# Attention operands stacked straight from the projection's SBUF tile, and the row of maxima put by ScalarE's queue

## The reference

```python
def proj(x, W, b):
    y = jnp.einsum('bsd,de->bse', x, W) + b
    return y.reshape(B, S, N_HEADS, D_K).transpose(0, 2, 1, 3)
q = proj(Q, W_Q, b_Q); k = proj(K, W_K, b_K); v = proj(V, W_V, b_V)
scores = jnp.einsum('bhqd,bhkd->bhqk', q, k) / jnp.sqrt(jnp.float32(D_K))
attn = jax.nn.softmax(scores, axis=-1)
out = jnp.einsum('bhqk,bhkd->bhqd', attn, v)
...
x = x + jnp.tanh(g_xattn[0]) * _L0_xattn_ref(_layernorm(x), ctx_1024, ctx_1024, W_Q, b_Q, ...)
x = x + jnp.tanh(g_ffn[0]) * _L0_ffn_ref(_layernorm(x), w_gate, w_up, w_down)
x = x + jnp.tanh(g_xattn[1]) * _L1_xattn_ref(_layernorm(x), ctx_1024)
x = x + jnp.tanh(g_ffn[1]) * _L1_ffn_ref(_layernorm(x), weight, bias, delta_w, delta_act)
```

## Time and profile before

| | |
|---|---|
| median of three runs | 1622.26 us |
| the profiled execution | 1623.71 us, with a span of 1621.9 us |
| TensorE busy (matmul) | 1477.0 us, 91% |
| VectorE busy | 1226.8 us, 76% |
| ScalarE busy | 875.9 us, 54% |
| GpSimd busy | 890.9 us, 55% |
| mean granted TensorE clock | 0.958 |
| bytes moved by DMA | 265.32 MB |

### The profile page before, as it was taken

How to read it: one execution, slowest core, us unless ns; L and a number is a source line. 1 busy time by engine, 2 the same in 40 slices (tenths; PEclk the granted TensorE clock), 3 DMA queues, 4 the chain that set the end, 5 groups by cost and what they waited for, 6 DMA issues and landing times. The chain is left out here.

```text
span 1621.9 us, 24716 instructions
## 1 busy us (share of the span) xinstructions
PE 1477.0 (91%) x6993; PEld 937.9 (58%) x6993; DVE 1226.8 (76%) x2135; ACT 875.9 (54%) x1433; POOL 890.9 (55%) x1148
## 2 busy tenths in 40 slices
PE   5699999999999889899784999999999968999997
PEld 3466666556565566655532455555555447887885
DVE  4867677777868677677662788888888848999986
ACT  4156666666565556555453555555555535555552
POOL 3166676585675757656462343343333316777775
PEclk9899999999999989999878999999999989999998
DMA  6757849485694865937941344444444653556522
GB/s 201 227 163 211 258 150 273 143 249 161 185 277 128 229 190 176 289 108 226 251 115 55 95 114 109 109 116 107 107 107 109 190 146 120 167 165 203 166 86 62
DMA packets 252172, 265.32 MB, mean 164 GB/s; under 512 B 139932, under 2 KB 162984, under 8 KB 247720
## 3 DMA queue, kind: packets, MB, share of 16 engines
q1 hardware_dynamic: 252072, 264.14, 57.4%
HBM read 149.50 MB, written 82.87 MB: 143 GB/s over the span
## 5 line engine op out<-in xcount | busy, mean ns | idle before, releaser
L724 ACT ACTIVATE a_probs<-a_sc 128x512 f32<-128x512 f32 x512 | 300.5, 595 | 288.5 <-PE a_sc L608 284.7
L843 DVE TENSOR_REDUCE a_negmax<-a_mx 128x1 f32<-128x512 f32 x512 | 339.0, 675 | 108.1 <-PE a_mx L591 107.3
L938 POOL TENSOR_TENSOR a_acc<-a_acc,a_probs 128x512 f32<-128x512 f32 x248 | 311.6, 1285 | 11.1 <-ACT a_probs L724 9.7
L938 POOL TENSOR_TENSOR a_acc<-a_probs 128x512 f32<-128x512 f32 x124 | 156.9, 1285 | 247.9 <-ACT a_probs L724 247.0
L591 PE MATMUL a_mx<-a_stack 96*128 96x512 f32 x512 | 231.0, 451 | 40.3 <-DVE a_negmax L843 22.3
L1089 PE MATMUL bank<-wcode,b_xq 128*128 128x512 bf16 x1024 | 229.3, 383 | 11.1 <-DMA b_xq<-b_xcode 11.1
L608 PE MATMUL a_sc<-a_stack 97*128 97x512 f32 x512 | 217.7, 427 | 21.0 <-DMA a_stack<-a_mrow 19.5
L1089 PEld LDWEIGHTS bank<-wcode,b_xq 128*128 128x128 bf16 x1024 | 100.5, 98 | 135.0 <-DMA b_xq<-b_xcode 12.5
L854 DVE RECIPROCAL a_attn<-a_den 128x128 f32<-128x128 f32 x128 | 120.8, 947 | 71.1 <-PE a_den L646 58.6
L591 PEld LDWEIGHTS a_mx<-a_stack 96*128 96x128 f32 x512 | 103.1, 201 | 114.4 <-DVE a_negmax L843 55.0
L1127 ACT ACTIVATE b_sig<-bank,b_tok 128x512 f32<-128x512 f32 x128 | 87.4, 683 | 94.0 <-PE bank L1089 91.9
(11 more groups left out here) (165 smaller groups left out, 2637.0 us busy)
## 6 DMA issues: line engine op xcount, KB each, us to landing
a_stack<-spill SPq DMA_DIRECT2D x192, 256.0 KB, 6.8
spill<-k_part SPq DMA_DIRECT2D x64, 512.0 KB, 3.5
ctx_t<-k_wo SPq DMA_DIRECT2D x16, 1024.0 KB, 9.8
c_ct<-ctx_t SPq DMA_DIRECT2D x8, 2048.0 KB, 7.9
a_stage<-in_x_dram SPq DMA_DIRECT2D x32, 256.0 KB, 5.1
a_stage<-in_ctx_dram SPq DMA_DIRECT2D x32, 256.0 KB, 3.1
a_wsum<-in_L_ffn_w_gate_dram SPq DMA_DIRECT2D x8, 1024.0 KB, 6.1
attn_t<-a_attn SPq DMA_DIRECT2D x32, 256.0 KB, 4.6
```

Source lines behind the costliest of these rows:

```text
L724: nc.scalar.activation(probs[:, k, j, :], sc[i % 2][:], ACT.Exp, scale=SCALE).then_inc(exp_done, 1)
L843: nc.vector.tensor_reduce(negmax[:, g % 2, j, t:t + 1], mx[i % 2][:], axis=AX.X, op=ALU.max, negate=True).then_inc(mx_done, 1)
L938: nc.gpsimd.tensor_tensor(acc[:, j], probs[:, 0, j] if k == 1 else acc[:, j], probs[:, k, j], ALU.add)\
```

## The change

The columns of W_Q and W_K are permuted inside each block of 128 when the weights are split, from (j r) to (r j), head j and dimension r. Partition p of a projection then holds dimension p // 4 of head p % 4, so that `part` read partition by partition is already in the order in which a stack's rows stand. The biases of Q and K are permuted alike: ScalarE copies the loaded block with the same permutation to a second one, and TensorE turns both. V is as it was.

With that a fill reads `part` in SBUF directly, and the spill with its DRAM tensor and semaphores is gone. The fills stand earlier in the clock. ScalarE may overwrite `part` once the fill of the group before has landed (before: once its spill had). The DMA of the maxima is issued by ScalarE's queue, not SP's, at the same tick.

```diff
+        def permuted(n, h):
+            to = w["qkv"[n]][:, :, h, :]
+            src = probs[:, n].rearrange("p a b -> p (a b)").rearrange("p (c e) -> p c e", c=C)
+            if n == 2:
+                return to, src
+            return (to.rearrange("p c (g r j) -> p c g r j", g=G, j=J), src.rearrange("p c (g j r) -> p c g r j", g=G, j=J))
-        brow = mrow[0:3 * G, 0, :].bitcast(F32)
+        brow, bpart = (mrow[0:3 * G, n, :].bitcast(F32) for n in range(2))
-        fill_at = {(0, Q): 17, (0, K): 25, (1, Q): 32, (1, K): 37, (2, Q): 41, (2, K): 46, (3, Q): 52, (3, K): 56}
+        fill_at = {(0, Q): 12, (0, K): 22.8, (1, Q): 27.4, (1, K): 32, (2, Q): 36.6, (2, K): 41.2, (3, Q): 49, (3, K): 50.4}
-                ck.add(ahead(qk_at[g, side] + 1.15 * (C - 1)) + at["spill"], 9, "spill", g, side)
# SP
-                    elif name == "spill":
+                    elif name == "fill":
                         g, side = args
                         sync_wait(sp, held, qk_lo, it, shift, 2 * G, 2 * g + side + 1)
-                        sync_wait(sp, held, stacked[g][side], it, shift, 1, 0, 48)
-                        sp.dma_start(spill[g, side].rearrange("h p s -> p h s"), part[:, side].bitcast(F32))\
-                            .then_inc(spilled[side], 16)
-                    elif name == "fill":
-                        g, side = args
-                        sync_wait(sp, held, spilled[side], it, shift, G, g + 1, 16)
                         sync_wait(sp, held, s_full, it, shift, G * T * J, (g - G + 1) * T * J)
                         for n, h in enumerate((HI, LO, HI) if side == Q else (HI, HI, LO)):
-                            sp.dma_start(stack[DH * n:DH * (n + 1), g, side].bitcast(F32),
-                                         spill[g, side, h].rearrange("(j r) s -> r j s", j=J))\
+                            sp.dma_start(stack[DH * n:DH * (n + 1), g, side].bitcast(F32), part[:, side, h].bitcast(F32))\
                                 .then_inc(stacked[g][side], 16)
-                    elif name == "mrow":
-                        g, = args
-                        sync_wait(sp, held, mt_done, it, shift, G, g + 1)
-                        sp.dma_start(stack[96:97, g, Q].bitcast(F32), mrow[:, g % 2, :].bitcast(F32))\
-                            .then_inc(mrow_put[g % 2], 16)
# TensorE
+                    pe.wait_ge(bias_put, 1)
+                    nc.tensor.transpose(den[:, 3 * G:6 * G], bpart[:], ident[0:3 * G, 0:3 * G])
                     nc.tensor.transpose(den[:, 0:3 * G], brow[:], ident[0:3 * G, 0:3 * G]).then_inc(bias_turned, 1)
# ScalarE
-                    nc.scalar.activation(w["qkv"[n]][:, :, HI, :], probs[:, n], ACT.Copy).then_inc(w_hi, 1)
+                    to, at_n = permuted(n, HI)
+                    nc.scalar.activation(to, at_n, ACT.Copy).then_inc(w_hi, 1)
-                    nc.scalar.activation(bias[:].rearrange("p n g -> p (n g)"), den[:, 0:3 * G], ACT.Copy).then_inc(bias_done, 1)
+                    nc.scalar.activation(flat[:, 0:2 * G], den[:, 3 * G:5 * G], ACT.Copy).then_inc(bias_done, 1)
+                    nc.scalar.activation(flat[:, 2 * G:3 * G], den[:, 2 * G:3 * G], ACT.Copy).then_inc(bias_done, 1)
-                        wait_count(act, spilled[side], it, shift, G, g, 16)
+                        wait_count(act, stacked[(g - 1) % G][side], it, shift, 1, 1 if g else 0, 48)
                         nc.scalar.activation(part[:, side, HI, :], turns.bank("qk", g, side)[:], ACT.Identity,
                                              bias=bias[:, side, g:g + 1]).then_inc(qk_hi, 1)
+                        if it + shift == 0 and i == T - 1:
+                            act.wait_ge(bias_loaded, 48)
+                            nc.scalar.activation(bpart[:].rearrange("n (r j) -> n r j", j=J), brow[:].rearrange("n (j r) -> n r j", j=J),
+                                                 ACT.Copy).then_inc(bias_put, 1)
+                    elif name == "mrow":
+                        g, = args
+                        wait_count(act, mt_done, it, shift, G, g + 1)
+                        nc.scalar.dma_start(stack[96:97, g, Q].bitcast(F32), mrow[:, g % 2, :].bitcast(F32))\
+                            .then_inc(mrow_put[g % 2], 16)
# VectorE
-                    nc.vector.tensor_tensor(w["qkv"[n]][:, :, LO, :], probs[:, n], w["qkv"[n]][:, :, HI, :].bitcast(F32),
-                                            ALU.subtract).then_inc(w_lo, 1)
+                    (to, at_n), (high, _) = permuted(n, LO), permuted(n, HI)
+                    nc.vector.tensor_tensor(to, at_n, high.bitcast(F32), ALU.subtract).then_inc(w_lo, 1)
```

More of the change, by code:

```diff
@@ L175, in wait_free, with attention_phase @@
             n -= len(self.banks)
-def attention_phase(nc, NB, keep0, keep1, x, ctx_in, w_q, b_q, w_k, b_k, w_v, b_v, spill, attn_t, ctx_t, ffn_w, w_o, b_o, weight, delta_w,
+def attention_phase(nc, NB, keep0, keep1, x, ctx_in, w_q, b_q, w_k, b_k, w_v, b_v, attn_t, ctx_t, ffn_w, w_o, b_o, weight, delta_w,
                     delta_act, g_xattn, g_ffn, w1_code, code_t):
@@ L283, in attention_phase @@
         w_loaded, w_hi, w_lo = [sem(f"w_loaded_{n}") for n in "qkv"], sem("w_hi"), sem("w_lo")
-        wv_lo, bias_turned, bias_done, ln_nmean = sem("wv_lo"), sem("bias_turned"), sem("bias_done"), sem("ln_nmean")
+        wv_lo, bias_put, bias_turned, bias_done, ln_nmean = sem("wv_lo"), sem("bias_put"), sem("bias_turned"), sem("bias_done"), sem("ln_nmean")
         consts, bias_loaded, pool_consts = sem("consts"), sem("bias_loaded"), sem("pool_consts")
@@ L306, in attention_phase @@
         ct_stored = sem("ct_stored")
-        spilled = [sem("spilled_q"), sem("spilled_k")]
         stacked = [[sem(f"stacked{g}_{n}") for n in "qk"] for g in range(G)]
@@ L512, in window @@
                     elif name == "boload" and b == NB - 1:
-                        sp.wait_ge(spilled[Q], 16 * G * NB)
-                        sp.wait_ge(spilled[K], 16 * G * NB)
+                        sp.wait_ge(stacked[G - 1][Q], 48 * NB)
+                        sp.wait_ge(stacked[G - 1][K], 48 * NB)
                         sp.dma_start(bo, b_o.partition_broadcast(P)).then_inc(bo_loaded, 16)
@@ L558, in window @@
                                 pe.wait_ge(w_lo, side + 1)
-                                pe.wait_ge(bias_done, 1)
+                                pe.wait_ge(bias_done, 2)
                             n = T if side == Q else 2 * T
@@ L666, in put_biases @@
                     act.wait_ge(bias_turned, 1)
-                    nc.scalar.activation(bias[:].rearrange("p n g -> p (n g)"), den[:, 0:3 * G], ACT.Copy).then_inc(bias_done, 1)
-                    act.wait_ge(bias_done, 1)
+                    flat = bias[:].rearrange("p n g -> p (n g)")
+                    nc.scalar.activation(flat[:, 0:2 * G], den[:, 3 * G:5 * G], ACT.Copy).then_inc(bias_done, 1)
+                    nc.scalar.activation(flat[:, 2 * G:3 * G], den[:, 2 * G:3 * G], ACT.Copy).then_inc(bias_done, 1)
+                    act.wait_ge(bias_done, 2)
                 def window(it, shift, name, args):
@@ L821, in window @@
                             split_weight(1)
-                            dve.wait_ge(bias_done, 1)
+                            dve.wait_ge(bias_done, 2)
                         if it + shift == 0 and i == 2 * T - 1:
@@ L1770, in build_program @@
     NB, S, D = x.shape
-    spill = nc.dram_tensor("spill", [4, 2, 2, P, S], F32, kind="Internal").ap()
     attn_t = nc.dram_tensor("attn_t", [NB, D // P, P, S], F32, kind="Internal").ap()
@@ L1779, in build_program @@
         with ExitStack() as keep0:
-            weights = attention_phase(nc, NB, keep0, keep1, x, ctx_in, w_q, b_q, w_k, b_k, w_v, b_v, spill, attn_t, ctx_t,
+            weights = attention_phase(nc, NB, keep0, keep1, x, ctx_in, w_q, b_q, w_k, b_k, w_v, b_v, attn_t, ctx_t,
                                       (w_gate, w_up, w_down), w_o, b_o, w1, delta_w, delta_act, g_xattn, g_ffn, w1_code, code_t)
```

## The result

The changed kernel takes **1648.57 us** (median of 4 runs, 1645.3 to 1652.41); the kernel before, beside it, 1621.88. The ratio is 1.0156, 95% interval 1.0132 to 1.018: it is 1.6% slower, clear of the noise. The prediction was 1588 us (1574 to 1608), so its sign was wrong. The profiled execution has 1645.3 us, with a span of 1643.5.

The account below looks back on a forecast made before the run. TensorE was taken to bound the attention part, so gains come from its idle time. Terms -12.7 - 1.5 - 18.2 + 1.5 - 4.9 + 0.8 = -35.0 from 1622.3 gave 1587.3, stated as 1588 us, range 1574 to 1608.

Parts of the forecast that it names:

- The step that failed: Steady-state fills: a fill from SBUF was taken to land in 6.8 us like one from DRAM; bound 0 if 3 us slower.
- Landings should rather shorten: DMA queue, at the reuse of `part`: without the spills' 512 KB each, fills should land sooner; margin there 1.4 us.
- Steady fills, -12.7: TensorE's 11 "issue" waits before maximum matmuls: fills issued earlier without spills remove all, -12.7 us (0 to -12.7).
- The first fill, -1.5: TensorE's 4.98 us wait at 45.16: shrinks by about 3, limited by VectorE's quantising, taken as -1.5 us (0 to -5).
- The row, -18.2: TensorE's 19.5 us of waits for the row of maxima: issue from ScalarE saves 18.2 us (-10 to -21).
- ScalarE's issues, +1.5: 32 DMA issues of 0.515 us moved to ScalarE, mostly covered by its idle time: +1.5 us (0 to +16.5).
- The clock, -4.9: TensorE's clock falls after idle gaps, at 556, 569 and 672 us; without the gaps none expected, -4.9 us (0 to -15).
- The start, +0.8: Split of W_Q reading at a step of 32 elements, plus bias copy and transpose: +0.8 us (0.3 to 5).
- The engines' time in every row goes by elements: Weight splits at the start: the reason given for expecting nearly no penalty from strided reads; the upper bound was +4.2 us.
- `part` is held longer, 0: ScalarE's new wait before overwriting `part` until fills land: tightest margin 1.4 us, Q from group 2 to 3; cost 0.
- the rival with 0.08: ScalarE waits at both group 2 to 3 handovers if fills land in 12.5 us: +25, 1645 us; chance 0.08.
- The rival on slower fills, 1619 us with 0.06: Fills out of SBUF take 3 us more, keeping the 12.7 and adding 22 us of ScalarE waits: 1619 us; chance 0.06.

Follow-up runs that it names:

- run 1: DMAs alone, none of the kernel's work: a fill took 5.15 us from DRAM, 8.03 from 128 SBUF partitions, 5.69 from 32, 8.94 by heads.
- run 12: The changed kernel with one line different: a fill's three DMAs interleave their stack rows, DMA n writing n, n+3, ... n+93; 1593.25 us, ratio 0.9825.
- run 13: DMAs alone, 128 partitions to 32 rows 1, 2, 3, 4 apart: 3.91, 3.87, 2.86, 2.34 us; fills on neighbouring rows 8.01, three apart 5.31.
- run 16: DMAs alone, 128 partitions to 32 rows: 0 to 31 3.91 us, every second from 32 2.80, from 0 3.86; also pairs and DMAs from DRAM.
- run 7: The kernel before with the row of maxima issued by ScalarE's queue and group 1's K fill at slot 36, not 37; 1596.04 us, ratio 0.9821.
- run 2: The kernel before with only the DMA of the row of maxima moved from SP's to ScalarE's queue; 1606.38 us, ratio 0.9893.
- run 14: The changed kernel with interleaved stack rows (three apart) and the row of maxima back in SP's queue; 1592.13 us, ratio 0.982.
- run 3: The changed kernel with the row of maxima back in SP's queue; 1640.43 us, ratio 1.0113 against the kernel before.
- run 15: The changed kernel with interleaved stack rows and plain, unpermuted weight splits (output not the reference's); 1587.31 us, ratio 0.9788.
- run 5: Single SBUF-to-SBUF DMAs and copies alone, by step 1, 2, 4, 8, 32 elements: ScalarE reads 1.91, 2.04, 3.83, 3.88, 3.67 us.
- run 6: The changed kernel with every fill DMA reading 32 partitions of 8 KB of K weights in SBUF, so operands are wrong; 1598.96 us, ratio 0.9834.
- runs 9 and 10: The changed kernel with twelve DMAs a fill, each from 32 partitions to eight rows: four apart 1705.18 us, neighbouring 1752.06 us.

## Why the prediction was wrong, step by step

- **The step that failed** is "I take the fill's own 6.8, for its destination (32 partitions of 8 KB) and its 2 KB pieces stay". Both stay, but the fill's source becomes 128 partitions, and such a fill takes 8.03 us where the one from DRAM takes 5.15 (run 1), that is 2.9 more; my own bound had 3. It is source and destination together: from the same 128 partitions to rows three apart a fill takes 5.31 us (run 13), from 32 partitions to the old rows 5.69 (run 1). In the kernel it costs 55 us (run 12 against the change, one line). The median landing, on which the term rested, hardly moved (6.9). What moved is how long the DMA engines are held, and with it the late landings: the longest on the stack is 14.6 us (12.5 before), and the row's median went from 1.9 to 5.6. "Landings should rather shorten" failed with it, at the very fill where the margin was thin. The Trainium skill ("SBUF — State Buffer", section "Door 1: The DMA port swizzle") has the rule that I didn't weigh: partitions 0 to 63 are reached through 8 of 16 ports, those from 64 on through the other 8. The trace agrees in direction: 3.86 us below row 64, 2.80 on both sides of it (run 16). It isn't all of it, since each DMA of the 5.69 us fill writes to one side of 64 as well. The same page of the Trainium skill (section "Can I just issue two DMAs to hit both halves?") says that a second DMA on the other half brings next to nothing; the pairs agree, 5.95 and 5.95 us. Why a DMA from DRAM doesn't care (3.00 us below 64, 3.33 on both sides) no run here shows; that stays open.
- **Steady fills, -12.7.** The reading of the "issue" waits as late fills was right (run 7 takes those of group 1 away by putting that fill one slot earlier, run 12 all of them), and the earlier order works once the spills are gone. In the change 7.5 of the 12.7 were gained.
- **The first fill, -1.5.** It got +0.3 in the change, 5.24 us at 49.98; in run 12 the wait is 2.35 us at 46.83, which is -2.6.
- **The row, -18.2.** Run 2 measures -17 in the kernel before: the size was right there. But it is not a term that adds: run 14 has the gain without the move. In four of the six waits of before, SP stood in line for a spill to land (4.1 to 8.3 us), then issued a fill and only then the row. One of them, from the kernel before (the copy ends at 559.62, TensorE starts at 569.16):

```profile
554.81 0.37 SPq L456 DMA_DIRECT2D spill<-k_part  x1
...
559.35 0.27 ACT L713 ACTIVATE a_mrow<-a_den 16x128 fp32r<-16x128 f32 x1 [1.70 <-PE a_den L597]
...
563.66 1.26 SPq L464 DMA_DIRECT2D a_stack<-spill  x3
565.04 0.54 SPq L470 DMA_DIRECT2D a_stack<-a_mrow  x1
```

  The wait of the last batch is another matter. There the row stands behind transposes, which are still in SP's queue: with the row on SP it is 8.1 us in run 3 (before: 8.5) and 3.3 in run 14. In the change these 8.5 us were saved, and 19.3 us spent at 13 other waits. The Trainium skill's rule weighed here (issuers share the 16 engines) agrees with run 1: beside a fill the row lands after 4.0 us, alone after 1.8.
- **ScalarE's issues, +1.5.** Not to be seen: with the issues back on SP (run 14) the time is the same within the intervals.
- **The clock, -4.9.** Not in the change, where TensorE's busy time grew from 1477.0 to 1487.0 us with new gaps. In run 12 it is 1473.9, 3.1 less, but the mean granted clock is 0.956, not above the 0.958 of before. In windows of 5 us from 50 to 770 us it is under 0.85 in 16 before and in 13 in run 12: the falls at 555, 570 and 670 us are gone, while one in nearly every batch stays (395, 490, 590 us). So the reading of the earlier trace rows holds for these, and the size of the term isn't shown.
- **The start, +0.8.** Mis-sized. The rows of after against the earlier trace rows:

```profile
10.23 3.77 ACT L651 ACTIVATE k_wbuf<-a_probs 128x2048 fp32r<-128x2048 f32 x1 [0.49 <-DMA a_probs<-in_L_xattn_W_Q_dram]
...
14.03 3.73 DVE L806 TENSOR_TENSOR k_wbuf<-a_probs,k_wbuf 128x2048 fp32r<-128x2048 f32 x1 [5.89 <-ACT k_wbuf L651]
```

  1.91 became 3.77 us, 2.29 became 3.73. The first projection on TensorE starts at 22.46, before at 19.37, and run 15 gives the whole as 6 us. The upper bound (+4.2) and the Trainium skill's rule of 16-byte lines that stood beside it were nearer right: the copies of run 5 pay nearly nothing at a step of 8 bytes and the full price from 16 on. "The engines' time in every row goes by elements" was drawn from rows that all read without a step.
- **`part` is held longer, 0.** With slow fills this became the rival with 0.08: ScalarE waited 22.3 us, up to 6.4. Seven of the eight waits stand at K from group 2 to 3, one of the two handovers named, none at Q; and they go as its rule says: where the slowest of the fill's DMAs lands in 7.1 us there is none, with 9.1 one of 0.9, with 14.6 one of 6.4 (its bound was 8.2). Its 1645 us (1647 by its own +25) are close to the 1648.57 measured, but partly by luck: it counts 60 us of such waits and keeps the 35 gained, and both were less. Shown is that the wait goes with the form of the fill (2.1 us in run 6, 0.3 in run 12). What a second `part` would bring wasn't tried.
- **The rival on slower fills, 1619 us with 0.06.** Its condition (3 us more for a fill) is what run 1 measures, 2.9. Its price was too low, and its sum is off: 35 - 12.7 - 22 - 2.5 leaves -2, which is 1624, not 1619.

With the start at +6 in place of +0.8 my sum is -29.8, or 1592.5 us; run 12 has 1593.25. That closeness is in part luck, since the first fill brought more than its term, ScalarE's issues and the clock less. But the large terms are there in run 12's waits: -12.7 for late fills and -16.6 for the row. They were sound for a fill that lasts about as long as before (5.31 us alone against 5.15), and that of the change doesn't.

## What to carry to other kernels

A DMA's price depends on which partitions it starts from and ends on; a median landing doesn't show it, the share of the DMA engines over a stretch does, and a few lines of DMAs alone measure it before the kernel is built around it. Where a DMA goes from SBUF to SBUF and the order of a tile's rows is free, as in a contraction, spread each DMA's rows over the whole tile, on both sides of partition 64. A step that is late because its queue waits for something needs no other queue once that something is gone. And before a rebuild, try the small edits that the same waits suggest: one DMA on another queue and one fill a slot earlier brought as much (run 7, ratio 0.9821) as the rebuild with interleaved rows (run 12, 0.9825).

## What the runs showed that I had not expected

- One DMA of 256 KB from 128 partitions to 32 rows of SBUF: 3.9 us on rows all on one side of 64 (or 48 to 79, of which 16 lie on each side, 3.89), 2.80 on every second row from 32, 2.34 on every fourth from 0. Rows 48 to 79 gain nothing, so a block that merely straddles 64 isn't enough. This too agrees with the map in the Trainium skill ("SBUF — State Buffer", section "Door 1: The DMA port swizzle"): by it these 32 rows reach 8 ports, as rows 0 to 31 do, and every second row from 32 reaches 16. Every third and every fourth row from 0 reach 16 as well and take 2.86 and 2.34 us, so the count of ports isn't all of it; the rest stays open.
- Two such DMAs together take 5.95 us, wherever the second one goes.
- A copy that reads or writes fp32 with a step of 16 bytes or more takes 1.9 to 2.0 times as long on ScalarE, 1.6 times on VectorE, 1.3 times on GpSimd; a step of 8 bytes costs 7% at most (run 5).
- SP takes 0.60 us at the median to issue one of a fill's three DMAs within SBUF, 0.43 for one out of DRAM, and 0.67 for one from 32 partitions to 8 rows (runs 9 and 10). Twelve for a fill cost more than the form saves.
